# A Mamba layer in a two-layer graph kernel: which scan operands lie in PSUM, and how GpSimd's products are grouped

## What is computed

```python
# layer 0, for (x, W1) and (x2, W2)
ax = adj @ x;  h = ax + (1 + eps) * ax;  three times: h = relu(h @ W[i].T + b[i])
x = layernorm(x + concat(out1, out2) @ Wm.T + bm)
# layer 1
h = relu(adj @ x @ gcn_w + gcn_b);  h = layernorm(h) * ln_g + ln_b
xc, z = split(h @ w_in);  u = silu(causal_conv4(xc) + conv_b)      # 256 channels
dt, B, C = ...(u @ w_xp);  dt = softplus(dt @ w_dt + b_dt)          # B, C: 16 states
dA = exp(dt * A);  dBu = dt * B * u
hst = dA * hst + dBu  (over the 4096 nodes);  y = sum over states of hst * C
x = layernorm(x + (y + u * D_skip) * silu(z) @ w_out)
```

## Time and profile before

| | us |
|---|---|
| median of 3 runs | 1087.23 |
| lowest, highest | 1086.82, 1090.28 |
| the profiled execution | 1086.18 |
| its span | 1084.6 |
| VectorE busy | 995.6 |
| TensorE busy | 971.7 |
| ScalarE busy | 559.5 |
| GpSimd busy | 337.6 |

### The profile page before, as it was taken

The page is one execution under the profiler, slowest core; times in us unless marked ns, Lnnn a source line. Parts: engine busy times, 40 slices in busy tenths (PEclk is TensorE's granted clock), DMA queues, the critical chain, the costliest instruction groups (busy, mean ns, idle before and its releaser), DMA issues. The chain is left out here.

```text
span 1084.6 us, 13272 instructions
## 1 busy us (share of the span) xinstructions
PE 971.7 (90%) x4134; PEld 671.6 (62%) x4134; DVE 995.6 (92%) x735; ACT 559.5 (52%) x1110; POOL 337.6 (31%) x228
## 2 busy tenths in 40 slices
PE   2889999999999999999998998989989999877665
PEld 2667777777777777634554564655646556445554
DVE  5989999999999999771999999999999999999996
ACT  3343343434343434225583875767847758477342
POOL 5450202020202021100532634426335263253652
PEclk9899999999999999999999999999999999988566
DMA  9999999999999999963825535365164452211200
GB/s 255 259 267 312 332 310 347 324 345 321 355 324 343 324 341 343 225 213 140 309 98 212 213 103 195 142 215 213 61 223 165 175 179 83 97 68 68 99 1 20
DMA packets 190396, 233.72 MB, mean 215 GB/s; under 512 B 8880, under 2 KB 164592, under 8 KB 175760
## 3 DMA queue, kind: packets, MB, share of 16 engines
q1 hardware_dynamic: 105936, 163.60, 46.3%
q10 hardware_dynamic: 80896, 60.57, 20.8%
q0 software_dynamic: 3520, 9.04, 2.8%
HBM read 170.00 MB, written 63.18 MB: 215 GB/s over the span
## 5 line engine op out<-in xcount | busy, mean ns | idle before, releaser
L958 DVE STREAM_TRANSPOSE at<-rows 128x1024 f32<-128x1024 f32 x136 | 267.8, 2011 | 21.9 <-DMA rows<-in_adj 7.5
L546 POOL TENSOR_TENSOR dBuP<-dtu,b_sb 128x1024 f32<-128x1024 f32 x77 | 182.9, 2376 | 282.1 <-DVE dtu L1074 115.1
L1223 PE MATMUL yT<-ah,xh 128*128 128x512 f32 x512 | 212.3, 415 | 34.8 <-DVE al L966 27.0
L599 ACT ACTIVATE ah<-at 128x2048 fp32r<-128x2048 f32 x64 | 122.6, 1915 | 211.4 <-PE yT L1223 196.1
L1310 PE MATMUL bank<-adjc,xm 128*128 128x512 f32 x448 | 206.0, 595 | 0.8 <-ACT axT L680 0.8
L1223 PE MATMUL yT<-al,xh 128*128 128x512 f32 x512 | 202.1, 395 | 0.0
L1223 PE MATMUL yT<-ah,xl 128*128 128x512 f32 x512 | 201.9, 394 | 0.0
L1420 PE MATMUL yT<-ident,pr 128*128 128x128 f32 x1008 | 147.4, 294 | 37.7 <-DVE pr L1139 31.2
L1420 PEld LDWEIGHTS yT<-ident,pr 128*128 128x128 f32 x1008 | 128.1, 152 | 67.9 <-DVE pr L1139 45.6
L834 ACT ACTIVATE dA<-dt,A_sb 128x512 f32<-128x512 f32 x182 | 122.6, 711 | 43.0 <-DVE dt L1071 43.0
L1139 DVE TENSOR_TENSOR pr<-hs,bank 128x1024 f32<-128x1024 f32 x112 | 134.3, 1199 | 11.2 <-PE bank L1402 11.0
(11 more groups left out here) (187 smaller groups left out, 1190.0 us busy)
## 6 DMA issues: line engine op xcount, KB each, us to landing
adjT<-at SPq DMA_DIRECT2D x56, 1024.0 KB, 7.5
adjc<-adjT SPq DMA_DIRECT2D x56, 1024.0 KB, 5.3
rows<-in_adj SPq DMA_DIRECT2D x152, 256.0 KB, 8.3
rows<-in_adj ACTq DMA_DIRECT2D x136, 256.0 KB, 8.7
b_sb<-b_dram ACTq DMA_DIRECT2D x37, 512.0 KB, 4.9
xm<-in_x SPq DMA_DIRECT2D x4, 512.0 KB, 10.7
res<-in_x POOLq DMA_DIRECT2D x8, 256.0 KB, 7.1
mid<-xn POOLq DMA_DIRECT2D x8, 256.0 KB, 7.9
```

What stands on the lines that cost most here:

```text
L546: nc.gpsimd.tensor_tensor(dBu(n, par)[:, :, 1:], dtu[par][:, :, :], b_sb[load % 2][:, nB(n) % 2:nB(n) % 2 + 1, :].to_broadcast([P, H, TILE ...
L599: nc.scalar.activation(ah[c % 2][:, :], at[c % 2][:, :, :].rearrange("p m t -> p (m t)"), ACT.Copy)\
L958: last = nc.vector.transpose(dst.rearrange("p m (g i) -> p g m i", i=32), src.rearrange("p g (i m) -> p g m i", i=32))
L1223: last = mm(acc[k][:, :], w[:, b, :], v[c % 2][:, cols], start=(b == 0 and j == 0), stop=(b == KB - 1 and j == 2))
```

## The change

The sets of states in PSUM change. States 0, 2 and 4 (`WHOLE_IN_BANK`) have both halves of their exponentials in PSUM, in M1 and `bank[6]`. States 5 and 6 have the first half there as before. States 1 and 3, which had one half in PSUM, are now in `CARRIED`: both halves in SBUF and one scan instruction. State 0 leaves `CARRIED`. The two banks are written again when the scan before last has ended (state 0's second half when the last product with C of the window before has).

GpSimd's products of 1 and 2 start when the scans of the window before are over, those of 3 and 4 behind scan 1, those of 5 and 6 behind scan 3. States 2 and 5 get a buffer of VectorE's (`dBuV`) as a third one. The power moves from behind product 5 to behind product 4 (`pool_rs`), and on ScalarE the statistics (`act_fs`) from n = 4 to 3, the skip term from 2 to 1, the copies of y from 3 to 2. On TensorE the turning of hn waits for scan 4 in place of the first half of scan 3. Line numbers behind the edits of the tables grow by up to 3.

```diff
--- before.py
+++ after.py
@@ -36,21 +36,22 @@
 
 
 
-AT = dict(pool_rs=5, pool_tail_rs=13, dve_dt=14, act_hn=5, act_hT=6, act_silu=11, act_bc=13,
+AT = dict(pool_rs=4, pool_tail_rs=13, dve_dt=14, act_hn=5, act_hT=6, act_silu=11, act_bc=13,
           act_sp=14, act_exp=14, act_ts=13, act_tail=15, dve_bc=11, dve_sp=14, dve_gate=1, pe_gcn=2, pe_gtr=3, pe_tr=6,
-          pe_z=9, pe_dbc=10, pe_dt=11, pe_turn=2, pe_out=9, act_b0=15, act_ax=2, act_g=2, act_fs=4,
-          act_start=1, act_skip=2, act_y=3)
+          pe_z=9, pe_dbc=10, pe_dt=11, pe_turn=2, pe_out=9, act_b0=15, act_ax=2, act_g=2, act_fs=3,
+          act_start=1, act_skip=1, act_y=2)
 FILL = (1, 1, 6, 1, 0, 0, 0, 9, 8)
 CONV = (0, 0, 0, 0, 0, 0, 0, 4, 4, 0, 0, 0, 0, 0, 0, 0)
 PLAN = (2, 4, 1, 2, 3, 3, 3, 0, 0, 0, 0, 2, 3, 3, 3, 3)
 AHEAD = sum(PLAN[AT['pe_gcn']:])
 C_IN_O = (0, 2, 4, 6)
 POOL = (1, 2, 3, 4, 5, 6, 7, 9, 11, 13, 15)
-IN_BANK = (1, 2, 3, 4, 5, 6)
+WHOLE_IN_BANK = (0, 2, 4)
+IN_BANK = (0, 2, 4, 5, 6)
 CARRIED = tuple(k for k in range(S) if k not in IN_BANK)
 B_LOADS = ((1, 2), (3, 4), (5, 6), (7, 9), (11, 13), (15,))
 B_LOAD_AT = {3: 2, 5: 3, 8: 4, 11: 5}
-POOL_AFTER = {n: 2 if n <= 7 else 3 for n in POOL}
+POOL_BEHIND = {1: -1, 2: -1, 3: 1, 4: 1, 5: 3, 6: 3, 7: 5, 9: 6, 11: 8, 13: 10, 15: 12}
 SUM_AFTER = 3
 LATE = (S - 2, S - 1)
 
@@ -276,7 +277,8 @@
         turns = {5: [("C", 1), ("C", 3), ("C", 5), ("C", 7), ("C", 8), ("B", 12), ("C", 11), ("C", 12), ("C", 14)],
                  6: [("B", 8), ("B", 10), ("C", 9), ("C", 10), ("B", 14), ("C", 13), ("C", 15)]}
         bank_of = {it: k for k in turns for it in turns[k]}
-        dA_bank = {1: M1, 2: bank[6], 3: M1, 4: bank[6], 5: bank[6], 6: bank[6]}
+        dA_bank = {(0, 0): M1, (0, 1): bank[6], (2, 0): M1, (2, 1): bank[6], (4, 0): bank[6], (4, 1): M1,
+                   (5, 0): bank[6], (6, 0): bank[6]}
 
         def spread_bank(kind, n):
             return M0 if (kind, n) == ("B", 0) else bank[4] if kind == "C" and n in C_IN_O else bank[bank_of[kind, n]]
@@ -284,11 +286,12 @@
         def dve_slot(n, par):
             return (n - nB(n) + NVB * par) % 2
 
-        def pool_slot(n, par):
-            return (nB(n) + NPB * par) % 2
-
         def dBu(n, par):
-            return dBuP[pool_slot(n, par)] if n in POOL_B else dBuV[dve_slot(n, par)]
+            if n in (2, 5):
+                return dBuV[dve_slot(8, par)]
+            if n in POOL_B:
+                return dBuP[par if n in (1, 4, 7, 11, 15) else 1 - par]
+            return dBuV[dve_slot(n, par)]
 
         LAST = TILES - 1
         last_dA = ((bank[7], bank[6]), (M0, M1))
@@ -541,7 +544,7 @@
                     if n in POOL_B:
                         load = nB(n) // 2
                         pool.wait_ge(b_in[load % 2], 16 * (len(B_LOADS) // 2 * b + load // 2 + 1))
-                        wait(pool, scanned, S * b + n - POOL_AFTER[n] + 1 if n > 1 else S * b)
+                        wait(pool, scanned, S * b + POOL_BEHIND[n] + 1)
                         pool.wait_ge(dtu_ready, b + 1)
                         nc.gpsimd.tensor_tensor(dBu(n, par)[:, :, 1:], dtu[par][:, :, :],
                                                 b_sb[load % 2][:, nB(n) % 2:nB(n) % 2 + 1, :].to_broadcast([P, H, TILE]),
@@ -824,14 +827,14 @@
                         if n == 0:
                             act.wait_ge(dt_ready, b + 1)
                         wait(act, scanned, S * b + n - NDA + 1)
-                        if n == 2:
-                            wait(act, C_multiplied, S * b)
-                        elif n == 3:
-                            act.wait_ge(half_scanned, len(IN_BANK) * b + 1)
-                        elif 4 <= n <= 6:
-                            act.wait_ge(half_scanned, len(IN_BANK) * b + (2 if n == 4 else n - 1))
+                        if n in (2, 4):
+                            act.wait_ge(scanned, S * b + n - 1)
+                        elif n in (5, 6):
+                            act.wait_ge(half_scanned, len(IN_BANK) * b + n - 2)
                         for h in range(H):
-                            nc.scalar.activation(dA_bank[n][:, :] if n in IN_BANK and h == 0 else dA[n % NDA][:, h, 1:], dt_[par][:, h, :], ACT.Exp,
+                            if n == 0 and h == 1:
+                                wait(act, C_multiplied, S * b)
+                            nc.scalar.activation(dA_bank[n, h][:, :] if (n, h) in dA_bank else dA[n % NDA][:, h, 1:], dt_[par][:, h, :], ACT.Exp,
                                                  scale=A_sb[:, h, n:n + 1]).then_inc(dA_ready, 1)
                     first = n - AT['act_start']
                     for k in range(first, S if n == S - 1 else min(first + 1, S - 1)):
@@ -1121,11 +1124,10 @@
                         wait(dve, state_kept, S * b + k - NHS + 1)
                         wait(dve, C_multiplied, S * b + k - NHS + 1)
                         if k in IN_BANK:
-                            last = nc.vector.tensor_tensor_scan(hs[k % NHS][:, 0, 1:], dA_bank[k][:, :], dBu(k, par)[:, 0, 1:],
-                                                                state[:, k, 0:1], ALU.mult, ALU.add)
-                            last.then_inc(half_scanned, 1)
-                            nc.vector.tensor_tensor_scan(hs[k % NHS][:, 1, 1:], dA[k % NDA][:, 1, 1:], dBu(k, par)[:, 1, 1:],
-                                                         state[:, k, 1:2], ALU.mult, ALU.add).then_inc(scanned, 1)
+                            nc.vector.tensor_tensor_scan(hs[k % NHS][:, 0, 1:], dA_bank[k, 0][:, :], dBu(k, par)[:, 0, 1:],
+                                                         state[:, k, 0:1], ALU.mult, ALU.add).then_inc(half_scanned, 1)
+                            nc.vector.tensor_tensor_scan(hs[k % NHS][:, 1, 1:], dA_bank[k, 1][:, :] if k in WHOLE_IN_BANK else dA[k % NDA][:, 1, 1:],
+                                                         dBu(k, par)[:, 1, 1:], state[:, k, 1:2], ALU.mult, ALU.add).then_inc(scanned, 1)
                     if k in CARRIED:
                         dve.wait_ge(start_set, len(CARRIED) * b + CARRIED.index(k) + 1)
                         flat = [a[:, :, :].rearrange("p h t -> p (h t)") for a in (hs[k % NHS], dA[k % NDA], dBu(k, par))]
@@ -1330,7 +1332,7 @@
 
             def front_tr(a):
                 pe.wait_ge(f_normed, RG * (a + 1))
-                wait(pe, half_scanned, len(IN_BANK) * (a - 1) + 3)
+                wait(pe, scanned, S * (a - 1) + 5)
                 for q in range(RG):
                     last = nc.tensor.transpose(M1[:, P * q:P * q + P], hn[:, q, :], ident[:, :])
                 last.then_inc(h_turned, 1)
```

## The result

| | us |
|---|---|
| before, median of 4 runs | 1087.57 |
| after, median of 4 runs (lowest, highest) | 1106.87 (1105.06, 1108.76) |
| ratio, 95% interval | 1.0164 (1.0143 to 1.0185) |
| the profiled execution after, its span | 1108.76, 1107.1 |
| VectorE busy before, after | 995.6, 986.6 |

What follows compares the result with a forecast made beforehand. VectorE's own queue was taken as the scan stage's clock. Windows, gains less waits for start copies, summed to +13.8 us; the B load's +2.3 made +16.1 on 1086.2, so 1102.3, range 1095 to 1110.

Steps and rivals of the forecast that it cites:

- VectorE's gain: VectorE's scan stage: shorter steps and no power collision at state 5 save 10.1 us over seven windows.
- surcharge for PSUM: VectorE's PSUM half scans: priced like SBUF ones; the skill's 0.065 us more each, 0.9 over seven windows, was left out.
- State 1: Before scan 1, window 1: VectorE waits 0.45 us for ScalarE's start copy behind state 2's exponentials.
- State 3: Before scan 3, window 1: VectorE idles 2.98 us for ScalarE's start copy; low end 0.9, high end 3.5.
- the price of the steps of ScalarE's chain that end on TensorE: ScalarE between the two start copies: axT 594.55 to 595.15, ReLU till 597.0, y's halves till 598.75 in window 1.
- C spreads of states 2 to 5: VectorE's waits for TensorE's spreads: nothing added, as TensorE runs ahead in idle time; uncovered, up to 1 us a window.
- The load of B: Load for states 7 and 9 behind exponential 5: late landings delay product 7 into state 6's SBUF half, +2.3 us (0 to 7).
- rival 1: Start columns of states 1 and 3 in time or nearly, not slower: 1083 us, or 1076 without any wait; chance 0.09.
- a short overlap: GpSimd product reaching into a VectorE SBUF half: costs little under 0.3 us of overlap, measured 0.09 taken.

Runs made afterwards that it cites:

- both copies first: Changed kernel with the start copies of states 1 and 3 right behind their own state's exponentials on ScalarE: 1085.58 us, ratio 0.997 to the kernel before.
- the changed kernel run again: The changed kernel, unedited, measured once more beside other runs on the same chip: 1103.94 us, ratio 1.0136 to the kernel before.
- the longer chain: Changed kernel with the first half of state 3's exponentials cut in four pieces on ScalarE: 1113.21 us, ratio 1.0219 to the kernel before.
- the pairs alone: Kernel before with only GpSimd's products in pairs and the third buffer for states 2 and 5, old banks kept: 1092.88 us, ratio 1.0043.
- y behind the statistics: Changed kernel, start copies 1 and 3 behind own exponentials, B load (states 7, 9) at n = 4, y copies behind statistics: 1099.61 us, ratio 1.0092.
- the earlier load: Changed kernel, start copies 1 and 3 behind own exponentials, B load (states 7, 9) at n = 4: 1085.29 us, ratio 0.9956; again 1087.39, 0.998.

## Why the prediction came out

It said 1102.3, from 1095 to 1110, slower; measured were 1106.87 and, in another set of runs, 1103.94.

- **VectorE's gain** (10.1 us over seven windows): the busy time fell by 9.0. The PSUM pair is 1.28 and 1.26, so no surcharge for PSUM showed: the SBUF half after them is 1.26 too. The Trainium skill (VectorE: DVE Perf Modes, the TRN2 errata) would make a PSUM half 0.065 longer by an estimate from its cycles; no such step is there.
- **State 1** (0.45): 0.54, 0.48 four times, 0.54. Window 0 waits 1.60 there, but from scan 0 to product 0, which waits for TensorE in both kernels, it is 8.6 us against 8.5: hidden, as forecast.
- **State 3** (2.98 in window 1, 2.95 in window 0): 2.76 and 2.86. In windows 2 to 5 the forecast has 3.2; it was 2.93 once and 3.94 or 3.95 three times. Scans 1 and 3 together: forecast 24.0, measured 25.4. The run with both copies first takes it all away.
- **What failed** is the price of the steps of ScalarE's chain that end on TensorE, as "axT ... released by TensorE; now 594.55 to 595.15, behind the copy": they were priced at TensorE's full clock, which the rows of before had. In three of the windows 2 to 5 the granted clock at scan 0 is 0.68 to 0.75, so part of the time at 1.2 in place of 2.4 GHz, and scan 3 waits 1.0 us more. From gate to gate such windows are 74.4 to 74.6 long, the others of windows 2 to 5 72.3; beyond scan 3 they wait for the spread of state 5 (0.43 to 0.44), at scan 7 (0.42 to 0.50) and for one later spread 0.73 to 0.82 in place of 0.44 to 0.47. The other profile of the same kernel has two such windows and a span of 1101.3, 16.7 over before; there window 2 is 72.33 against my 70.15 + 2.3 = 72.45. The rest of what parts the two profiles lies in window 1, 1.3 us longer in the first (at 609 to 617 us its clock is 0.75 and 0.82, in the second 1.00), and in window 6, 2.6 us longer.
- **C spreads of states 2 to 5** (nothing): of these only state 5's is late, 0.37 to 0.44 in windows 1, 2, 3 and 5 of the first profile. The waits for all spreads grow from 11.0 to 14.2 there, and in the second profile they are 10.2. "TensorE uses the idle time to run ahead" holds where the clock does; in window 6 of the first profile, at a clock of 0.79 from 985 to 1005 us, two spreads are 1.84 and 1.06 late, which are 0.38 and in time in the second. Before has them 1.08 and 1.05 late, behind a stretch at 0.57, so this is not the change's doing alone.
- **The load of B** (+2.3): not there. The landing times that I took, 3.8 to 5.8 against a budget of 4.6, belong to a kernel in which the load runs beside the adjacency's. In after they are 3.4 to 4.0, because the wait before scan 3 pulled the two apart: while the load of states 7 and 9 was in flight in window 2, the adjacency's queue moved 1.02 MB in before, nothing in after, and 1.11 MB with both copies first. This load alone in window 2 (count, KB, us from issue to landing), in the same three runs:

```profile
b_sb<-b_dram ACTq DMA_DIRECT2D x1, 512.0 KB, 4.5
```

```profile
b_sb<-b_dram ACTq DMA_DIRECT2D x1, 512.0 KB, 3.8
```

```profile
b_sb<-b_dram ACTq DMA_DIRECT2D x1, 512.0 KB, 5.1
```

The term belongs to the kernel without the stall. There the load lands after 5.0 to 5.6 us in windows 0 to 5, which costs VectorE 4.4 us, and rival 1's 1076 to 1083 came out as 1085.6.
- **The sum.** Against the first profile (span +22.5) the forecast is short by 6.4, against the second (+16.7) by 0.6. But two slow-clocked windows cost the second some 4.4 (2 x 2.2), and the load that it was spared was put at 2.3. So without the clock I would have been 4 us too high, or 3 if before is freed of its one such window too (window 5, 0.8 us longer than window 4). That the number is so close is in part luck: misses of opposite sign.

What stays open: why the clock falls in window 2 of one execution and not of the other. The work ahead of it is the same in both: TensorE waits 1.55, 1.24 and 1.18 us for VectorE's products in one and 1.55, 1.24 and 1.17 in the other. Before shows it too, among windows 1 to 6 at scan 0 of window 5 alone (0.72). That more idling of VectorE makes it more frequent is not shown either. One step speaks for it: two windows of six in the changed kernel run again, three in its first profile, six with the longer chain. Two speak against it: with the pairs alone, 4 us slower than before, there are four (0.70 to 0.79 in windows 3 to 6), and with y behind the statistics, where VectorE waits 14 us more for C spreads than in the run with the earlier load, there is one. No run takes the idling of TensorE alone away.

## What to carry to other kernels

When an operation is switched to a form that needs one more small input, ask where in its producer's in-order queue that input is made, and count the work between it and its release, waits included: here a copy of 0.2 us behind an exponential pair and the statistics cost 1.6% of the whole kernel. Take transfer times from a kernel in which the same transfers lie beside each other; a stall moves them apart or together. And where a chain of waits passes through TensorE, read its granted clock window by window, in more than one execution: here a window with a slow start cost 2.2 us more, and the same kernel had two of them in one profile and three in the other.

## What the runs showed of the hardware

The forecast took it that a short overlap of a GpSimd product and a VectorE scan from two SBUF inputs costs little and a long one all of it. The rows give one rule for both. If the product has started first, the scan grows by the overlap less 0.18 or 0.19: 0.28 gives 0.10 (the half at 595.33 of the earlier trace rows and the product below), 0.97 gives 0.79 (both copies first, window 2), 1.19 gives 1.01, 2.14 gives 1.95 (the pairs alone). If the scan has started first, it loses nothing and GpSimd waits, 4.37 in place of 2.37 at an overlap of 2.21.

```profile
593.24 2.37 POOL L546 TENSOR_TENSOR dBuP<-dtu,b_sb 128x1024 f32<-128x1024 f32 x1 [2.31 <-DVE hs L1132]
```

The Trainium skill (SBUF — State Buffer, "Who interferes with whom") has both the exclusion and that the order in which the two are issued decides which one blocks, and these rows agree. The prediction used the first half alone, and the expectation for the pairs priced every overlap as VectorE's loss. The 0.2 us that the second one does not pay is from these rows.

The power of four columns follows the same rule. It is 1.01 long beside PSUM scans or an idle VectorE. In window 1 of before it is 1.92: it starts at 606.35, behind the SBUF half of state 4, which ends at 607.47, so an overlap of 1.12 gives 0.91.
